# Second layer's cross attention: the key mask added by VectorE instead of by TensorE products

## The chip, the cores and the metric

The kernel runs on one core of a Trainium2 chip. The metric is the device time of one execution in microseconds (us). The engines are TensorE (PE in the profile, with its weight loads listed apart as PEld), VectorE (DVE), ScalarE (ACT), GpSimd (POOL) and SyncE (SP). SBUF is the working memory with 128 partitions, PSUM the memory that TensorE writes its results to.

## The reference, cut to what matters

The program is a decoder of two layers for 32 sequences of 64 tokens with 256 features, 2048 tokens in all. Each layer has an attention or state space part, a cross attention and a part with experts, each followed by a residual sum and a normalization. The change touches the cross attention of the second layer alone:

```python
def _L1_xattn_ref(hidden_states, memory_tokens, memory_mask, norm_w, wq, wk, wv, wo, wg):
    scale = HD ** (-0.5)                       # 16 heads of 16 features
    x = rmsnorm(hidden_states, norm_w)
    q = (x @ wq.T).reshape(B, L, NH, HD)
    k = (memory_tokens @ wk.T).reshape(B, M, NH, HD)
    v = (memory_tokens @ wv.T).reshape(B, M, NH, HD)
    attn = jnp.einsum('blhd,bmhd->bhlm', q, k) * scale
    attn = jnp.where(memory_mask[:, None, None, :], attn, -jnp.inf)
    attn = jax.nn.softmax(attn, axis=-1)
    attn = jnp.nan_to_num(attn, nan=0.0)
    out = jnp.einsum('bhlm,bmhd->blhd', attn, v).reshape(B, L, C)
    out = out @ wo.T
    gate = jax.nn.sigmoid(x @ wg.T)
    return gate * out
```

The key mask has one entry for each sequence and key (32 x 64). It is the same for all 16 heads and all queries of a sequence.

## The kernel before, in words

The parts of the decoder run one after the other, each in a block of its own that all engines leave together. `layer1_cross_attention` works on 16 tiles of 128 tokens, two sequences each. The scores of a tile are 128 x 1024 float32: a query in each partition, and along the columns 16 heads of 64 keys. They fill two banks of PSUM (`eps_s`), of which there is one copy only, so the scores of the next tile can't be written before those of this one have been read.

The order is written out by hand as a software pipeline. `for s in range(SLOTS)` runs over 22 slots on each engine, and slot `s` holds work on tiles of several ages. On TensorE a slot is: scores of tile s-1 (`scores`), queries and keys of tile s (`queries_keys`, `eps_qk`), the transposes of the mixed values of s-4 (`turn_y`), the transposes of the attention weights of s-2 (`weights`, `eps_pt`), values and gate of s (`values_gate`, `eps_vg`), the mixing of values of s-3 (`mix`, `eps_y`), the output projection of s-4 (`output`, `eps_o`) and the transposes of the normalized rows of s-5 back to feature order (`turn_back`). Slots 1 to 16 have scores, and 17 to 21 drain the pipeline.

On VectorE a slot is `softmax` of s-1 (maximum L2293, a floor under it L2295, the subtraction L2299), `apply` of s-5 (normalization L2305), `quotient` of s-3 (L2311 to L2317) and `sums` of s-4 (L2325 to L2333). On ScalarE: `turned_out` of s-6 (L2224), `exps` of s-2 (exponential L2231), the queries and keys out of PSUM for s (L2238, L2241), the turned weights out for s-2 (L2247), the mixed values out for s-4 (L2253), a square for s+1 (L2220) and values and gate out for s (L2262, L2266). GpSimd takes powers of -1/2 for the two normalizations (L2190, L2199). All engines but TensorE's weight load go strictly in order, and a semaphore stands wherever one engine takes what another made.

The mask is a bfloat16 tile `e_neg` (128 x 16 tiles x 64 keys) made once at the start (L2339): 0 for a key that counts and -1e30 for one that doesn't. In `scores` two products with the identity write it into the two banks, 512 columns each, repeated over the heads (L2381), and eight products of queries and keys (L2386) accumulate onto it. `eps_s` is released by the semaphore `shifted` of the subtraction, since maximum and subtraction both read it. `e_sm` (two copies, SBUF, float32) holds the subtracted scores until the exponential has read them.

Of the kernel before, what the change touches and what calls it, by code (L numbers as in the profile page):

```python
# [20 lines left out]
ALU = mybir.AluOpType  # L21
ACT = mybir.ActivationFunctionType
AX = mybir.AxisListType
ds = bass.ds

P = 128
B, T, D = 32, 64, 256
# [34 lines left out]
class Kernel:  # L62
# [23 lines left out]
    def sem(self, name):  # L86
        self.sems.append(self.nc.alloc_semaphore(name=name))
        return self.sems[-1]
# [2051 lines left out]
def layer1_cross_attention(k, w):  # L2140
# [4 lines left out]
    nc, io, sem = k.nc, k.io, k.sem  # L2145
    RMS_EPS, FLOOR, TINY = 1e-6, -1e20, 1e-30
    PAIRS, GD = HEADS // 2, 2 * (HD + 1)
    with ExitStack() as ctx:
# [7 lines left out]
        neg = sb("neg", [P, TILES, T], BF16)  # L2156
# [3 lines left out]
        sm, mx, pr, pt = many(2, "sm", [P, 16, T]), many(2, "mx", [P, 16]), many(2, "pr", [P, 8, P]), many(2, "pt", [P, 8, P])  # L2160
        total, yn, yT = many(2, "total", [P, 16]), many(2, "yn", [P, 16, HD]), many(2, "yT", [P, KD, P])
        r, stats, mv, rstd = many(2, "r", [P, D]), many(2, "stats", [P, 6]), many(2, "mv", [P, 2]), many(2, "rstd", [P, 1])
        qk_ps, vg_ps = k.ps("eps_qk", [P, 4, P], F32, ctx), k.ps("eps_vg", [P, 2, D], F32, ctx)
        s_ps, pt_ps = k.ps("eps_s", [P, 2, 512], F32, ctx), k.ps("eps_pt", [P, 8, P], F32, ctx)
# [2 lines left out]

        pre_done, squared, biased, fac_done = sem("e_pre_done"), sem("e_squared"), sem("e_biased"), sem("e_fac_done")
        vbd_zero, vbd_set = sem("e_vbd_zero"), sem("e_vbd_set")
        qk_full, qT_out, kbd_out = sem("e_qk_full"), sem("e_qT_out"), sem("e_kbd_out")  # L2170
        vg_full, vg_out = sem("e_vg_full"), sem("e_vg_out")
        s_full, max_done, floored, shifted, exped = sem("e_s_full"), sem("e_max_done"), sem("e_floored"), sem("e_shifted"), sem("e_exped")
# [7 lines left out]
        def live(t):  # L2180
            return 0 <= t < TILES

        with nc.Block() as block:
# [103 lines left out]
            @block.vector  # L2287
            def _(dve):
                def softmax(t):
                    v = t % 2  # L2290
                    s = s_ps[:].rearrange("p r (h s) -> p (r h) s", s=T)
                    dve.wait_ge(s_full, t + 1)
                    dve.tensor_reduce(mx[v][:], s, AX.X, ALU.max).then_inc(max_done, 1)  # L2293
                    dve.wait_ge(max_done, t + 1)
                    dve.tensor_scalar(mx[v][:], mx[v][:], FLOOR, None, ALU.max).then_inc(floored, 1)  # L2295
                    dve.wait_ge(floored, t + 1)
                    if t >= 2:
                        dve.wait_ge(exped, t - 1)
                    dve.tensor_tensor(sm[v][:], s, mx[v][:].unsqueeze(2).broadcast_to([P, 16, T]), ALU.subtract).then_inc(shifted, 1)  # L2299

                def apply(t):
                    v = t % 2
                    dve.wait_ge(rstd_done, t + 1)
                    dve.wait_ge(squared, min(t + 2, TILES))
                    dve.tensor_scalar(k.resid[:, t, :], r[v][:], mv[v][:, 0:1], rstd[v][:], ALU.subtract, ALU.mult).then_inc(rn_done, 1)  # L2305

                def quotient(t):
                    v = t % 2
                    y = y_ps[:, 0:16 * (HD + 1)].rearrange("p (h d) -> p h d", d=HD + 1)
                    dve.wait_ge(y_full, t + 1)  # L2310
                    dve.tensor_scalar(total[v][:], y[:, :, HD], TINY, None, ALU.max).then_inc(total_done, 1)  # L2311
                    dve.wait_ge(total_done, t + 1)
                    dve.reciprocal(total[v][:], total[v][:]).then_inc(rc_done, 1)
                    dve.wait_ge(rc_done, t + 1)
                    if t >= 2:
                        dve.wait_ge(y_turned, t - 1)
                    dve.tensor_tensor(yn[v][:], y[:, :, 0:HD], total[v][:].unsqueeze(2).broadcast_to([P, 16, HD]), ALU.mult).then_inc(y_out, 1)  # L2317

                def sums(t):
                    v = t % 2  # L2320
                    dve.wait_ge(o_full, t + 1)
                    dve.wait_ge(vg_out, 3 * (t + 1))
                    if t >= 2:
                        dve.wait_ge(rn_done, t - 1)
                    dve.scalar_tensor_tensor(r[v][:], gate[t % 6][:], 1.0, o_ps, ALU.add, ALU.mult).then_inc(o_out, 1)  # L2325
                    dve.wait_ge(o_out, t + 1)
                    dve.tensor_tensor(r[v][:], r[v][:], k.resid[:, t, :], ALU.add).then_inc(r_done, 1)
                    dve.wait_ge(r_done, t + 1)
                    dve.bn_stats(stats[v][:], r[v][:]).then_inc(stats_done, 1)
                    dve.wait_ge(stats_done, t + 1)  # L2330
                    if t >= 2:
                        dve.wait_ge(rstd_done, t - 1)
                    dve.bn_aggr(mv[v][:], stats[v][:]).then_inc(mv_done, 1)  # L2333

                dve.wait_ge(k.ahead_in, 16 * len(k.ahead))
                for kd in range(KD):
                    dve.tensor_scalar(wq[:, kd, :], wq[:, kd, :], nw[:, kd:kd + 1], 0.5, ALU.mult, ALU.mult).then_inc(pre_done, 1)
                    dve.tensor_scalar(wg[:, kd, :], wg[:, kd, :], nw[:, kd:kd + 1], None, ALU.mult).then_inc(pre_done, 1)
                dve.tensor_scalar(neg[:], mask8[:], -1.0, BIG, ALU.add, ALU.mult).then_inc(pre_done, 1)  # L2339
                dve.tensor_scalar(wo[:], wo[:], 0.5, None, ALU.mult).then_inc(pre_done, 1)  # L2340
                for s in range(SLOTS):
                    if live(s - 1):
                        softmax(s - 1)
                    if live(s - 5):
                        apply(s - 5)
                    if live(s - 3):
                        quotient(s - 3)
                    if live(s - 4):
                        sums(s - 4)

            @block.tensor
            def _(pe):
# [22 lines left out]
                def scores(t):  # L2375
                    pe.wait_ge(kbd_out, 4 * (t + 1))
                    pe.wait_ge(qT_out, t + 1)
                    if t >= 1:
                        pe.wait_ge(shifted, t)
                    for r2 in range(2):  # L2380
                        pe.matmul(s_ps[:, r2, :], k.identb[:], neg[:, t, :].unsqueeze(1).broadcast_to([P, 8, T]), start=True, stop=False)  # L2381
                    for r2 in range(2):
                        rows = slice(r2 * 64, r2 * 64 + 64)
                        for hh in range(2):
                            for b in range(2):
                                ins = pe.matmul(s_ps[b * T:(b + 1) * T, r2, hh * 256:(hh + 1) * 256],  # L2386
                                                qT[t % 2][rows, hh, b * T:(b + 1) * T],
                                                kbd[t % 2][rows, hh * 2 + b, :, :].rearrange("p h s -> p (h s)"),
                                                start=False, stop=(hh == 1))
                    ins.then_inc(s_full, 1)  # L2390

                def weights(t):
# [677 lines left out]
```

## Time and profile before

| | us |
|---|---|
| median of three runs | 1281.39 |
| lowest and highest | 1274.37, 1285.85 |
| the profiled execution | 1271.11 |
| its span, first to last instruction | 1269.0 |
| busy in it: TensorE | 1112.9 (88%) |
| VectorE | 781.2 (62%) |
| ScalarE | 575.9 (45%) |
| GpSimd | 455.1 (36%) |

The mean granted clock of TensorE is 0.958 of full speed. The busy times are those of one profiled execution; an engine with a small share may still be the one that the others wait for in one part of the program. The part with the cross attention of the second layer takes from about 828 to 985.87 us of the span. In the rows further down, "x16" counts instructions, and "idle before <-" is the time in which the engine had nothing to do just before the instruction, with what released it.

### The profile page before, as it was taken

To read this page: it belongs to the slowest core of one execution; us is meant where nothing else is said; L and a number is where in the kernel's file an instruction comes from. 1 tells how busy PE (TensorE), PEld (TensorE's weight loads), DVE (VectorE), ACT (ScalarE), POOL (GpSimd) and SP (SyncE) were. 2 spreads that over 40 slices of the span, in tenths; PEclk is the share of its full clock that TensorE was granted. 3 is DMA by queue.
4 is the path that set the end of the run, shared out by engine and by line. 5 is a ranking of instruction groups with operands and counts; after the bars stand their busy time and mean duration, and the time that the engine had idled before them with its cause. 6 is when DMAs were issued, how large, how long until landed. Compare 5 with 4: busy or idle time off the path is not lost. (4 is left out here: it accounts for less than half of the span.)

```text
span 1269.0 us, 20972 instructions
## 1 busy us (share of the span) xinstructions
PE 1112.9 (88%) x7484; PEld 662.5 (52%) x7484; DVE 781.2 (62%) x1531; ACT 575.9 (45%) x1199; POOL 455.1 (36%) x692
## 2 busy tenths in 40 slices
PE   6888779988888588999579998789998899999997
PEld 3566544454443245776234455567786343545455
DVE  4889887888884322333667677736566355555554
ACT  2666516766677301333455664256664322122120
POOL 6999852545542263333224445421111000000001
PEclk7999969999999799999789999989999899999999
DMA  6658244655652023333323000000000000000000
GB/s 217 202 174 275 81 124 122 150 137 148 146 130 53 25 84 96 105 109 101 99 65 141 1 1 1 1 1 2 2 2 1 25 1 0 9 9 9 8 9 25
DMA packets 73115, 91.72 MB, mean 72 GB/s; under 512 B 12691, under 2 KB 61997, under 8 KB 72333
## 3 DMA queue, kind: packets, MB, share of 16 engines
q1 hardware_dynamic: 68595, 80.72, 22.6%
q0 software_dynamic: 3408, 9.34, 2.1%
q8 instruction: 62, 1.02, 0.4%
q10 hardware_dynamic: 1010, 0.31, 0.1%
q14 instruction: 40, 0.33, 0.1%
HBM read 55.37 MB, written 29.17 MB: 67 GB/s over the span
## 5 line engine op out<-in xcount | busy, mean ns | idle before, releaser
L919 ACT ACTIVATE a_late<-a_qkv 128x512 f32<-128x512 f32 x128 | 77.2, 603 | 58.9 <-PE a_qkv L996 58.9
L2546 POOL TENSOR_SCALAR f_rstd<-f_mv 128x1 f32<-128x1 f32 x16 | 3.8, 240 | 267.9 <-DVE f_mv L2685 267.8
L867 DVE TENSOR_REDUCE b_nm<-a_s 128x4 f32<-128x1024 f32 x64 | 78.0, 1219 | 29.9 <-PE a_s L965 29.8
L2630 DVE TENSOR_TENSOR f_prod<-f_sg,f_kept 128x512 f32<-128x512 f32 (+1 forms) x48 | 33.2, 692 | 97.9 <-ACT f_kept L2575 95.0
L2755 PE MATMUL fps_h<-residT,w_f_w 128*128 128x512 f32 x176 | 83.9, 617 | 2.4 <-DVE f_inner L2667 2.4
L867 DVE TENSOR_REDUCE b_nm<-a_pt 128x4 f32<-128x1024 f32 x64 | 76.7, 1198 | 1.5 <-PE a_pt L965 1.5
L919 ACT ACTIVATE a_late<-a_y 128x512 f32<-128x512 f32 x128 | 76.9, 600 | 0.0
L2569 ACT ACTIVATE f_sg<-fps_h 128x512 f32<-128x512 f32 (+1 forms) x24 | 14.3, 596 | 126.6 <-PE fps_h L2774 109.8
L1011 PE MATMUL a_o<-a_late,b_vt 128*32 128x256 f32 x1024 | 69.2, 389 | 0.0
L1299 POOL DMA_INDIRECT routed<-c_out,c_target x39 | 37.5, 962 | 67.4 <-ACT c_out L1371 67.1
L1888 DVE SCALAR_TENSOR_TENSOR d_acc<-d_pad,d_cw,d_acc 128x512 f32<-128x512 f32 x72 | 57.8, 810 | 1.7
L351 POOL TENSOR_TENSOR a_nrm<-a_ss,phalf 128x20 f32<-128x20 f32 x16 | 57.0, 3560 | 4.2 <-DVE a_ss L473 4.2
L2755 PEld LDWEIGHTS fps_h<-residT,w_f_w 128*128 128x128 f32 x176 | 33.8, 196 | 42.9 <-issue 38.5
L1547 PE MATMUL cps_h<-c_wgu,c_xT 128*128 x156 | 52.7, 461 | 0.7 <-ACT c_xT L1359 0.6
L1486 DVE TENSOR_TENSOR c_hid<-c_sg,cps_h 128x176 f32<-128x176 f32 x39 | 13.2, 338 | 63.2 <-issue 50.6
L839 POOL TENSOR_TENSOR a_rest<-a_rest 128x256 f32<-128x256 f32 x16 | 11.6, 725 | 96.8 <-DVE a_rest L892 96.8
L1737 POOL TENSOR_TENSOR d_rs<-d_ms,mhalf 128x4 f32<-128x4 f32 x16 | 22.4, 1401 | 65.6 <-DVE d_ms L1945 65.6
L2011 PE MATMUL dps_ip<-residT,d_win 128*128 128x512 f32 x96 | 44.6, 598 | 0.3 <-ACT d_zs L1798 0.2
L1293 POOL DMA_INDIRECT xrows<-c_xr,c_place_int x32 | 31.1, 971 | 34.6 <-DVE c_xr L1456 19.3
L2569 ACT ACTIVATE f_sg<-f_kept 128x512 f32<-128x512 f32 (+1 forms) x24 | 15.1, 630 | 60.1 <-DVE f_kept L2635 60.1
L1566 PE MATMUL cps_o<-c_wd,c_hT 88*128 x156 | 40.1, 380 | 0.0
L1011 PEld LDWEIGHTS a_o<-a_late,b_vt 128*32 128x32 f32 x1024 | 26.9, 110 | 25.1 <-issue 14.0
(425 smaller groups left out, 2895.8 us busy)
## 6 DMA issues: line engine op xcount, KB each, us to landing
kparts<-a_rest SPq DMA_DIRECT2D x48, 192.0 KB, 3.2
a_rest<-a_rest SPq DMA_DIRECT2D x64, 128.0 KB, 3.1
xrows<-in_c_fill SPq DMA_DIRECT2D x13, 387.0 KB, 4.4
c_xrow<-xrows SPq DMA_DIRECT2D x39, 129.0 KB
c_back<-routed SPq DMA_DIRECT2D x16, 256.0 KB, 3.3
a_front<-kparts SPq DMA_DIRECT2D x12, 288.0 KB
a_front<-qparts SPq DMA_DIRECT2D x36, 96.0 KB
qparts<-b_xp SPq DMA_DIRECT2D x48, 64.0 KB, 2.8
```

Source lines behind the costliest of these rows:

```text
L351: gp.tensor_tensor(nrm[v][:], ss[v][:], k.phalf[:, 0:H20], ALU.pow).then_inc(rooted, 1)
L867: dve.tensor_reduce(nm[s % 2][:, 4 * n:4 * n + 4].rearrange("p (g h) -> p g h", h=2), s1[step % 2][:], AX.X, ALU.max, negate=True).then_in ...
L919: act.activation(pr[g % 8][:], s2[g % 2][:], ACT.Exp, scale=SCALE).then_inc(s2_out, 1)
L1011: ins = pe.matmul(o_ps[32 * j:32 * j + 32, q % 2, :], vt[x % 2][:, lh, g, :], pr[g % 8][:, lh, :], start=(lh == 0), stop=(lh == KD - 1))
L1293: gp.indirect_dma_start(k.xrows[:], bass.IndirectOffsetOnAxis(ap=place_int[n][:, t:t + 1], axis=0), xr[:, t, :], None).then_inc(scattered[ ...
L1299: gp.indirect_dma_start(routed[:], bass.IndirectOffsetOnAxis(ap=target[s % 8][:], axis=0), out[s % 4][:], None).then_inc(sent[s % 4], 16)
L1547: ins = pe.matmul(h_ps[s % 2][:, 0:2 * F], xT[s % 2][:, kd, :], wgu[:, kd, ds(e, 1), :].rearrange("p a f -> p (a f)"), start=(kd == 0), st ...
L1566: ins = pe.matmul(o_ps[:, s % 2, 0:D], hT[s % 2][:, c, :], wd2[:, ds(e, 1), c, :].rearrange("p a f -> p (a f)"), start=(c == 0), stop=(c = ...
L1888: ins = dve.scalar_tensor_tensor(out=acc[v][:], in0=pad[v][:, :, tap:tap + T], scalar=cw[:, m, tap:tap + 1], in1=acc[v][:], op0=ALU.mult, ...
L2011: ins = pe.matmul(bank[:], win[:, kd, m * P:(m + 1) * P] if m < XT else wz[:, kd, (m - XT) * P:(m - XT + 1) * P], k.residT[:, kd, c * CHUN ...
L2630: dve.tensor_tensor(prod[n % 2][at], sg[n % 2][at], up, ALU.mult).then_inc(prod_done, 1)
L2755: pe.matmul(h_ps[j][:], (w1, w3)[j][:, kd, m * P:(m + 1) * P], k.residT[:, kd, c * CHUNK:(c + 1) * CHUNK], start=(kd == 0), stop=False)
```

## The change

The two mask products of each tile go, and with them the accumulation: each product of queries and keys starts and ends its own sum. VectorE's `softmax` has a new first instruction, which reads the scores from PSUM, adds the mask repeated over the heads, and writes `e_sm`. The maximum is taken from `e_sm`, and the subtraction works in place on `e_sm`. A new semaphore `masked` is raised by the addition; TensorE waits for it, in place of `shifted`, before it writes the next scores. The wait for the exponential that last read this copy of `e_sm` moves from the subtraction to the addition.

```diff
         vbd_zero, vbd_set = sem("e_vbd_zero"), sem("e_vbd_set")
+        masked = sem("e_masked")
...
                 def softmax(t):
                     v = t % 2
-                    s = s_ps[:].rearrange("p r (h s) -> p (r h) s", s=T)
                     dve.wait_ge(s_full, t + 1)
-                    dve.tensor_reduce(mx[v][:], s, AX.X, ALU.max).then_inc(max_done, 1)
+                    if t >= 2:
+                        dve.wait_ge(exped, t - 1)
+                    dve.tensor_tensor(sm[v][:], s_ps[:].rearrange("p r (h s) -> p (r h) s", s=T),
+                                      neg[:, t, :].unsqueeze(1).broadcast_to([P, 16, T]), ALU.add).then_inc(masked, 1)
+                    dve.wait_ge(masked, t + 1)
+                    dve.tensor_reduce(mx[v][:], sm[v][:], AX.X, ALU.max).then_inc(max_done, 1)
                     dve.wait_ge(max_done, t + 1)
                     dve.tensor_scalar(mx[v][:], mx[v][:], FLOOR, None, ALU.max).then_inc(floored, 1)
                     dve.wait_ge(floored, t + 1)
-                    if t >= 2:
-                        dve.wait_ge(exped, t - 1)
-                    dve.tensor_tensor(sm[v][:], s, mx[v][:].unsqueeze(2).broadcast_to([P, 16, T]), ALU.subtract).then_inc(shifted, 1)
+                    dve.tensor_tensor(sm[v][:], sm[v][:], mx[v][:].unsqueeze(2).broadcast_to([P, 16, T]), ALU.subtract).then_inc(shifted, 1)
...
                     if t >= 1:
-                        pe.wait_ge(shifted, t)
-                    for r2 in range(2):
-                        pe.matmul(s_ps[:, r2, :], k.identb[:], neg[:, t, :].unsqueeze(1).broadcast_to([P, 8, T]), start=True, stop=False)
+                        pe.wait_ge(masked, t)
...
-                                                start=False, stop=(hh == 1))
+                                                start=True, stop=True)
```

On TensorE, around the scores of tile 7 in slot 8, the instructions stand like this before (output projection, transposes back, mask, scores, queries, keys):

```order
L2425 MATMUL eps_o<-w_e_wo,e_yT 128x256 x2
L2434 MATMUL eps_pt<-ident,resid 128x128 x2
L2381 MATMUL eps_s<-e_neg,identb 128x512 x2
L2386 MATMUL eps_s<-e_kbd,e_qT 64x256 x8
L2359 MATMUL eps_qk<-residT,w_e_wq 128x128 x4
L2359 MATMUL eps_qk<-ctxT_all,w_e_wk 128x128 x4
```

and like this after:

```order
L2426 MATMUL eps_o<-w_e_wo,e_yT 128x256 x2
L2435 MATMUL eps_pt<-ident,resid 128x128 x2
L2387 MATMUL eps_s<-e_kbd,e_qT 64x256 x8
L2362 MATMUL eps_qk<-residT,w_e_wq 128x128 x4
L2362 MATMUL eps_qk<-ctxT_all,w_e_wk 128x128 x4
```

The scores follow the transposes back directly; nothing else has moved.

On VectorE, at the same place, before (the last two of `sums`, then `softmax`, `apply` and the first of `quotient`):

```order
L2329 BN_STATS e_stats<-e_r 128x6
L2333 BN_AGGR e_mv<-e_stats 128x2
L2293 TENSOR_REDUCE e_mx<-eps_s 128x16
L2295 TENSOR_SCALAR e_mx<-e_mx 128x16
L2299 TENSOR_TENSOR e_sm<-eps_s,e_mx 128x1024
L2305 TENSOR_SCALAR resid<-e_r,e_mv,e_rstd 128x256
L2311 TENSOR_SCALAR e_total<-eps_y 128x16
```

and after:

```order
L2332 BN_STATS e_stats<-e_r 128x6
L2336 BN_AGGR e_mv<-e_stats 128x2
L2295 TENSOR_TENSOR e_sm<-eps_s,e_neg 128x1024
L2298 TENSOR_REDUCE e_mx<-e_sm 128x16
L2300 TENSOR_SCALAR e_mx<-e_mx 128x16
L2302 TENSOR_TENSOR e_sm<-e_sm,e_mx 128x1024
L2308 TENSOR_SCALAR resid<-e_r,e_mv,e_rstd 128x256
L2314 TENSOR_SCALAR e_total<-eps_y 128x16
```

The addition stands ahead of the maximum, and is now the only instruction that reads `eps_s`.

## Rows read from the trace of the kernel before

**Rows 1.** Windows: start:end, length, busy time per engine, granted clock, DMA share, GB/s.

```profile
core 0: us, PE busy (x) PEld busy (x) DVE busy (x) ACT busy (x) POOL busy (x), PEclk, DMA share, GB/s
837.25:964.87 127.62, 127.62 (x1434) 100.97 (x1433) 70.43 (x141) 85.73 (x203) 19.12 (x51) 1.00 0.01 2
965.90:985.87 19.97, 12.93 (x150) 9.47 (x147) 12.50 (x33) 6.39 (x13) 3.93 (x10) 1.00 0.00 1
985.87:989.00 3.13, 3.13 (x16) 0.66 (x16) 0.00 (x0) 0.00 (x0) 0.00 (x0) 0.50 0.64 217
989.00:1269.00 280.00, 267.25 (x764) 132.44 (x760) 150.98 (x279) 63.69 (x116) 12.90 (x32) 0.98 0.03 8
```

**Rows 2.** Timeline (start, length, engine, line) of TensorE around the mask, steady slots.

```profile
901.25 0.59 PE L2381 MATMUL eps_s<-e_neg,identb 128*128 128x512 bf16 x2
...
910.04 0.38 PE L2434 MATMUL eps_pt<-ident,resid 128*128 128x128 f32 x2
910.16 0.21 PEld L2381 LDWEIGHTS eps_s<-e_neg,identb 128*128 128x128 bf16 x2
...
910.26 0.59 PE L2381 MATMUL eps_s<-e_neg,identb 128*128 128x512 bf16 x2
...
910.79 0.65 PEld L2386 LDWEIGHTS eps_s<-e_kbd,e_qT 64*64 64x64 f32 x16 [0.42 <-issue]
```

**Rows 3.** Timeline of VectorE in the same slot.

```profile
909.20 0.17 DVE L2311 TENSOR_SCALAR e_total<-eps_y 128x16 f32<-128x16 f32 x1 [3.21 <-PE eps_y L2410]
...
911.62 0.18 DVE L2333 BATCH_NORM_AGGREGATE e_mv<-e_stats 128x2 f32<-128x6 f32 x1
...
911.98 1.23 DVE L2293 TENSOR_REDUCE e_mx<-eps_s 128x16 f32<-128x1024 f32 x1 [0.18 <-PE eps_s L2386]
...
914.59 0.40 DVE L2305 TENSOR_SCALAR resid<-e_r,e_mv,e_rstd 128x256 f32<-128x256 f32 x1
```

**Rows 4.** Groups of VectorE instructions by form: total us, mean ns, idle before.

```profile
L2656 DVE TENSOR_TENSOR f_hid<-f_aw 128x512 f32<-128x512 f32 x20 | 13.8, 690 | 0.6
...
L499 DVE TENSOR_TENSOR a_front<-a_front,a_sc 128x256 f32<-128x256 f32 x16 | 11.8, 738 | 0.0
...
L1392 DVE TENSOR_TENSOR c_acc<-cps_o,resid 128x1024 f32<-128x1024 f32 x4 | 4.9, 1213 | 5.6 <-PE cps_o L1528 5.6
```

**Rows 5.** Timeline in the fill: the exponential and the transposes that need it.

```profile
843.72 1.14 ACT L2231 ACTIVATE e_pr<-e_sm,e_fac 128x1024 f32<-128x1024 f32 x1
...
845.77 1.04 PE L2399 MATMUL eps_pt<-ident,e_pr 128*128 128x128 f32 x8
```

**Rows 6.** Timeline of slot 16 and of the drain behind it.

```profile
964.83 1.14 ACT L2231 ACTIVATE e_pr<-e_sm,e_fac 128x1024 f32<-128x1024 f32 x1
...
965.70 0.18 DVE L2333 BATCH_NORM_AGGREGATE e_mv<-e_stats 128x2 f32<-128x6 f32 x1
...
966.06 1.22 DVE L2293 TENSOR_REDUCE e_mx<-eps_s 128x16 f32<-128x1024 f32 x1 [0.18 <-PE eps_s L2386]
...
966.18 1.04 PE L2399 MATMUL eps_pt<-ident,e_pr 128*128 128x128 f32 x8
...
968.67 0.40 DVE L2305 TENSOR_SCALAR resid<-e_r,e_mv,e_rstd 128x256 f32<-128x256 f32 x1
...
969.57 0.38 PE L2434 MATMUL eps_pt<-ident,resid 128*128 128x128 f32 x2
...
970.27 1.14 ACT L2231 ACTIVATE e_pr<-e_sm,e_fac 128x1024 f32<-128x1024 f32 x1
...
971.47 1.09 PE L2399 MATMUL eps_pt<-ident,e_pr 128*128 128x128 f32 x8 [0.68 <-ACT e_pr L2231]
```

**Rows 7.** First attention, by source line (lengths in ns: least, median, most) and timeline.

```profile
L495 DVE TENSOR_TENSOR a_sc<-a_sc,a_factor x16: 167/643/649, 19.8 to 146.9; 128x20 f32<-128x20 f32 x16
...
102.71 0.80 POOL L362 TENSOR_TENSOR a_front<-a_front,a_rest 128x256 f32<-128x256 f32 x1
102.90 0.64 DVE L495 TENSOR_TENSOR a_sc<-a_sc,a_factor 128x20 f32<-128x20 f32 x1
```

## The prediction

> **What bounds the kernel now.** I looked at the windows by stage first, then at the timeline of one steady slot, then at where the pipeline fills and drains. The part that the change touches is the cross attention of the second layer, from about 828 us to 985.87 us. Between the first and the last score product TensorE is busy for 127.62 of 127.62 us, VectorE for 70.43 and ScalarE for 85.73, at full granted clock; after that the pipeline drains for 19.97 us, in which TensorE is busy for only 12.93 [rows 1]. So in the steady part TensorE's own instruction stream is the bound, and an instruction taken from it should shorten every slot. In the drain the bound is a chain that goes from engine to engine, and there VectorE's work counts.
>
> The timeline shows a steady slot: the mask products start at 901.25 and again at 910.26, so a slot is 9.01 us [rows 2]. Within it VectorE waits 3.21 us for the mixed values, and its last statistics of the slot end at 911.62 + 0.18 = 911.80, hardly before the maximum starts at 911.98 [rows 3]. The second number matters: scores that come earlier will not be picked up much earlier, since VectorE is still at work.
>
> **What is removed: two products of TensorE per tile, 32 in all.** The transposes back start at 910.04, the mask's weights at 910.16, its first product at 910.26, and the scores' first weights at 910.79 [rows 2]. Without the mask the scores can start where the mask started. From its first product that is 910.79 - 910.26 = 0.53 us, from its first weights 910.79 - 910.16 = 0.63. I take 0.53, because a first product there still has to have weights in the array, and the scores' first weights need to be loaded just as the mask's were. Below lies the case that the idle 0.42 us of the weight load ahead of the scores stays (it would then be a price of the switch to the small tiles of the scores, not of the mask): 0.63 - 0.42 = 0.21. The bounds are 0.21 and 0.63.
>
> The same row can be read another way. The Trainium skill, "TensorE: Matmul & The Clock Gate", section "Back-to-back issue gap", gives N/2.4 + 2.5 ns from one product's start to the next at full clock, so an estimate of 216 ns for each of these 512-column products and 0.43 for the two. By it the sum below would be 15 x 0.43 - 0.73 = 5.7 us of gain. The row has 0.53, which also holds the weight load that stands ahead, and I go by the row.
>
> **What is added on VectorE: one addition of 1024 columns per tile, 16 in all.** It reads the scores in PSUM and the mask in SBUF, and writes SBUF. The nearest row is a float32 sum of the same size with one operand in each memory, at 1213 ns [rows 4]; this trace has no row for a bfloat16 operand in such a sum, nor for one repeated over the heads. The highest price by a row is that of a product with a repeated operand, 738 ns for 256 columns [rows 4]; by the rows of 512 and 1024 columns an instruction costs 1.02 ns per column and 168 ns besides, so this one has (738 - 168)/256 = 2.2 ns per column, which for 1024 would be 2.45 us. At that price VectorE would still fit into the slot, and the drain alone would be 1.2 us longer. I take 1.22, and 0.04 for the semaphore behind it. Nothing below 1.2 is to be had. The maximum and the subtraction then read SBUF in place of PSUM. The 690 ns for 512 columns are those of a product with both operands in SBUF, and they lie on one line with the sum that has one in PSUM [rows 4]; I change nothing for them.
>
> VectorE in a slot is at work for 9.01 - 3.21 - 0.18 = 5.62 us. With the addition it is 5.62 + 1.26 = 6.88, and the slot of TensorE becomes 9.01 - 0.53 = 8.48. **So 1.6 us of idle VectorE remain in each slot**, and the addition is hidden. Who waits for VectorE there? The scores' PSUM is now free after the addition: that starts at about 911.85 and ends at 913.1, and the next scores come six microseconds later. The subtraction ends 1.1 us later than now, and behind it on VectorE's queue stands the normalization, now at 914.59 [rows 3], which the transposes back need only at the slot's end. None of it is late. The exponentials take the subtraction's result one slot later.
>
> What could come late on ScalarE is the exponential ahead of TensorE's transposes of the weights, since TensorE gains 0.53 between the two. In the fill, where it is tightest, it ends at 843.72 + 1.14 = 844.86, while TensorE's first transpose is at 845.77 and its weights 0.1 ahead of that [rows 5]. Of these 0.8 us, 0.53 go and 0.27 stay. In the steady slot there is more.
>
> **The drain.** In slot 16, the last with scores, two things are different. First, the exponential of tile 14 ends at 964.83 + 1.14 = 965.97 and the transposes start at 966.18 [rows 6], with their weights 0.1 earlier, so that TensorE can not use the sixteenth 0.53. Second, the chain now goes through VectorE: its statistics end at 965.88, the maximum starts at 966.06, the normalization at 968.67; behind that the transposes back at 969.57, behind these in ScalarE's queue the exponential at 970.27, and behind it the transposes at 971.47, where TensorE had waited 0.68 [rows 6]. With the addition ahead, everything from the maximum on is 1.26 later, less the 0.13 by which the addition starts earlier (965.93): 1.13. The normalization at 969.80 ends at 970.21, the transposes back start at 970.30 in place of 969.57, which is 0.73 later, and the exponential and the transposes with it. From there the drain keeps its form. So the drain costs 0.73.
>
> **The sum.** 15 x 0.53 - 0.73 = 7.95 - 0.73 = 7.2 us of gain. The profiled execution took 1271.11 us with a span of 1269.0, and would be 1263.9. The median of the three runs is 1281.39, 10 above it; that difference is the spread between executions, of which the three runs show 1274.37 to 1285.85. From the median I get 1281.4 - 7.2 = **1274 us**.
>
> **The rivals.**
>
> *The gap ahead of the scores stays.* For it: a gap of this size is put down to "issue" in the row, not to an engine [rows 2]. Against it: while that gap runs, two products of 512 columns are streaming. Gain 15 x 0.21 - 0.73 = 2.4 us, 1279 us. Chance 0.13. (Were that gap itself all that goes, and the mask's weight load found its like in the scores', it would be 15 x 0.42 - 0.73 = 5.6 us and 1276, which I count to the forecast.)
>
> *The clock is dealt anew.* Right behind the drain the granted clock is 0.50 for 3.13 us, the lower of its two levels, after a drain with TensorE at 65% busy; over the last 280 us it is 0.98 on average [rows 1]. The end of the drain is now stretched by 0.73 and everything later moves by 7 us, so a fall can come earlier, or once more. One more such stretch of dense products costs half its length, 1.6 us; two cost 3.1. The result would be 1276 to 1277, or as much better if one goes away. Chance 0.08.
>
> *VectorE becomes the bound.* This is the way to a slower kernel. Its place is the steady slot; it decides when the addition takes more than 8.48 - 5.66 = 2.8 us, and the kernel is slower than before only above 3.4 us in the slots, since a slot was 9.01. At 4.0 us a slot would be 9.66, and 13 slots cost 13 x 0.65 = 8.4, and the drain 4.04 - 0.13 - 0.41 = 3.5 more: 12 us, 1293. Against it: no row of this size is above 1.23, and even the worst row gives 2.45. Chance 0.03.
>
> *The subtraction, now with both operands in SBUF, is held up by GpSimd.* The first attention shows such a thing: a product of 128x20 with both operands in SBUF, which takes 167 ns at least, took 640 at 102.90, and ended just behind GpSimd's subtraction of 102.71 to 103.51 [rows 7]. The price here would be the length of GpSimd's operation, up to 0.8 us per tile by that row. VectorE has 1.6 us to spare in a slot, so it would be seen in the drain alone, once: gain 7.2 - 0.8 = 6.4, 1275. By my times the subtraction stands at 914.6 to 915.8, and GpSimd's power for this slot's normalization has ended by then, since VectorE's normalization at 914.59 waited for nothing [rows 3]. Chance 0.04. The Trainium skill, "SBUF — State Buffer", section "Who interferes with whom", states the rule behind it: a VectorE instruction with two SBUF inputs contends with a GpSimd instruction that reads SBUF, and the second waits in full. The rows agree. It speaks against this change, which turns a subtraction with one SBUF input into one with two.
>
> The rest, 0.72, is the forecast.
>
> **Numbers.** The costs alone give gains from 2.4 to 15 x 0.63 - 0.73 = 8.7, so 1273 to 1279; the clock adds 3 on either side. The larger part of the range is the spread of the executions, 11 us over three runs, half of which I allow to a median: 1265 to 1282. About 1% (13 us) is what a measurement of this kernel can tell from no change. A gain of 7 is 0.6%, so within 1% is by far the likeliest; more than 1% faster needs 6 us of luck in the executions, 0.14; more than 1% slower needs VectorE as the bound, 0.03.
>
> **What would show it.** In the profile of the changed kernel the starts of successive scores in the steady part should lie 8.48 us apart, with the scores' first weights directly behind the transposes back and no idle time of TensorE. The addition should read 1.22 us, VectorE's longest wait in a slot should fall from 3.21 to about 1.5, and stay for the mixed values. The drain should take some 20.7 us and not 19.97 from the end of the last scores, with TensorE waiting more for the last exponential. I am wrong if the slots are 8.8 us or more (the gap stayed), if TensorE waits in a steady slot for VectorE or ScalarE (a wait has taken the place of the products), or if the granted clock in the steady part is below 1.00.

## The result, and the profile after

The changed kernel takes 1272.42 us in the median of 20 runs (1267.85 to 1279.63), the kernel before 1277.82 in 20 runs on the same chips (1273.03 to 1286.44). The ratio is 0.996, with a 95% interval of 0.9943 to 0.9976: a gain of 0.4%, or 5.1 us, between 3.1 and 7.3. That is within 1% and in the range of 1265 to 1282, and below the 7.2 us of the forecast.

The spans of the two profiled executions, 1269.0 and 1268.4 us, don't show this. The stage's first product of queries starts at 830.23 before and at 834.35 after; over all profiled executions of this study it starts between 829.68 and 841.75, though no kernel changes the stages ahead of it. So I compare from that product on. Windows of the changed kernel: from the first product of queries to the first scores, to the last scores, to the first product of the experts, to the next products there, to the end.

```profile
core 0: us, PE busy (x) PEld busy (x) DVE busy (x) ACT busy (x) POOL busy (x), PEclk, DMA share, GB/s
834.35:840.88 6.53, 6.53 (x37) 5.75 (x38) 0.00 (x0) 2.24 (x7) 3.54 (x15) 0.60 0.01 3
840.88:961.90 121.02, 121.02 (x1403) 98.50 (x1402) 87.28 (x155) 85.53 (x201) 19.53 (x51) 1.00 0.01 2
961.90:984.10 22.20, 14.59 (x164) 9.95 (x164) 14.99 (x38) 7.73 (x14) 3.92 (x10) 0.97 0.00 1
984.10:987.67 3.57, 3.57 (x17) 0.65 (x17) 0.00 (x0) 0.00 (x0) 0.00 (x0) 0.50 0.62 220
987.67:1268.40 280.73, 268.08 (x764) 132.68 (x760) 151.04 (x279) 63.68 (x116) 12.84 (x32) 0.98 0.02 8
```

The same windows of the kernel before:

```profile
830.23:837.26 7.03, 7.03 (x39) 6.00 (x39) 0.00 (x0) 2.51 (x8) 4.04 (x15) 0.62 0.01 2
837.26:964.87 127.61, 127.61 (x1434) 100.96 (x1433) 70.43 (x141) 85.72 (x203) 19.11 (x51) 1.00 0.01 2
964.87:985.87 21.00, 13.96 (x163) 10.03 (x163) 13.45 (x36) 7.42 (x14) 3.93 (x10) 1.00 0.00 1
985.87:989.33 3.46, 3.46 (x16) 0.66 (x17) 0.00 (x0) 0.00 (x0) 0.00 (x0) 0.53 0.64 221
989.33:1269.00 279.67, 266.92 (x764) 132.44 (x760) 150.98 (x279) 63.69 (x116) 12.90 (x32) 0.98 0.02 8
```

The reader is to see three things. The stretch from the first to the last scores, 15 slots, is 6.59 us shorter, 0.44 per slot, and TensorE is still busy in all of it, while VectorE has 17 us more to do. The drain is 1.20 longer. The first stretch is 0.50 shorter, but that isn't to be put down to the change: it runs in part at the lower clock (0.60 and 0.62), and the kernel with products and addition further down, whose mask products are those of before, takes 6.16 us for it. So the stage takes 984.10 - 834.35 = 149.75 us in place of 155.64, 5.9 less, and what is behind it 1.2 more.

One steady slot of the changed kernel, TensorE and VectorE, in answer to [rows 2, 3]:

```profile
901.83 1.11 PE L2387 MATMUL eps_s<-e_kbd,e_qT 64*64 64x256 f32 x16
...
909.25 0.17 DVE L2314 TENSOR_SCALAR e_total<-eps_y 128x16 f32<-128x16 f32 x1 [1.80 <-PE eps_y L2411]
...
910.10 0.38 PE L2435 MATMUL eps_pt<-ident,resid 128*128 128x128 f32 x2
...
910.41 0.65 PEld L2387 LDWEIGHTS eps_s<-e_kbd,e_qT 64*64 64x64 f32 x16 [0.17 <-issue]
...
911.68 0.18 DVE L2336 BATCH_NORM_AGGREGATE e_mv<-e_stats 128x2 f32<-128x6 f32 x1
911.78 1.20 DVE L2295 TENSOR_TENSOR e_sm<-eps_s,e_neg 128x1024 f32<-128x1024 f32 x1
...
913.01 1.22 DVE L2298 TENSOR_REDUCE e_mx<-e_sm 128x16 f32<-128x1024 f32 x1
...
914.48 1.23 DVE L2302 TENSOR_TENSOR e_sm<-e_sm,e_mx 128x1024 f32<-128x1024 f32 x1
...
915.62 0.41 DVE L2308 TENSOR_SCALAR resid<-e_r,e_mv,e_rstd 128x256 f32<-128x256 f32 x1
```

A slot is 910.41 - 901.83 = 8.58 us. From the transposes back to the scores it is 0.31 us, where it was 0.75. The addition takes 1.20 us and starts right behind the statistics, and VectorE's longest wait has gone from 3.21 to 1.80.

### The profile page after: what moved, and what is told of

Read it like the earlier page. It is cut to its first block and busy times, and to the rows that moved or that the text cites. A ratio compares the mean times of both kernels' runs of the same rounds, so it can differ in the third digit from the quotient of the medians.

```text
span 1268.4 us, 20924 instructions
## 1 busy us (share of the span) xinstructions
PE 1113.3 (88%) x7452; PEld 663.0 (52%) x7452; DVE 801.8 (63%) x1547; ACT 575.7 (45%) x1199; POOL 453.0 (36%) x692
```

## The experiments

Each run's profile is read in the same four pieces. "Slots" is the time from the first to the last scores (15 of them), "drain" from the last scores to the experts' first product, "stage" from the first product of queries to the experts' first. All in us:

| kernel | slots | drain | stage | ratio to before |
|---|---|---|---|---|
| before | 127.62 | 21.00 | 155.64 | 1 |
| changed | 121.03 | 22.20 | 149.75 | 0.996 (0.9943 to 0.9976) |
| products and addition | 127.61 | 22.12 | 155.89 | 1.0004 (0.9976 to 1.0033) |
| neither | 121.03 | 21.58 | 149.17 | 0.9939 (0.9907 to 0.9971) |
| one product | 124.37 | 21.11 | 152.30 | one run |
| four products | 134.10 | 21.00 | 162.72 | one run |
| two additions | 121.04 | 27.17 | 154.84 | 1.0 (0.997 to 1.0029) |
| three additions | 126.97 | 27.68 | 161.10 | 1.0048 (1.002 to 1.0075) |
| two additions, spare products | 121.03 | 23.89 | 151.24 | 0.9969 (0.9946 to 0.9991) |
| changed, normalization earlier | 121.03 | 21.65 | 149.18 | 0.9964 (0.9939 to 0.999) |
| changed, spare products | 121.04 | 24.45 | 151.48 | 0.9936 (0.9912 to 0.996) |
| factor on the values | 121.22 | 21.33 | 149.27 | 0.9936 (0.9908 to 0.9965) |
| the same, nine spare products | 121.22 | 24.46 | 152.04 | 0.995 (0.9929 to 0.997) |
| the same, three spare products | 121.22 | 21.76 | 149.75 | 0.9938 (0.9915 to 0.996) |

### The two halves of the change apart

Both, the products back and the addition kept:

```diff
                         pe.wait_ge(masked, t)
+                    for r2 in range(2):
+                        pe.matmul(s_ps[:, r2, :], k.identb[:], neg[:, t, :].unsqueeze(1).broadcast_to([P, 8, T]), start=True, stop=False)
...
-                                                start=True, stop=True)
+                                                start=False, stop=(hh == 1))
```

> Changed kernel, but the two mask products of TensorE are put back ahead of the scores (the mask is then added twice). Theory (each slot is as long as TensorE's own stream, and the addition costs in the drain alone): slots of 9.01 us as in the kernel before, from the last scores to the next stage 21.0 + 0.76 = 21.8 us, the whole stage 156.4 us against 155.6 before; about 0.8 us slower than before, not to be told from no change. Rival (the addition lengthens the slots as well, and the products are worth more than 0.43 us): slots of 9.2 us or more, 3 us slower or more.

The slots take 127.61 us, as before to the hundredth, with VectorE doing the addition in each of them. The drain is 1.12 longer than before, where 0.8 was expected, and the time is that of before (1.0004). About 0.25 of the 1.12 stand at its end, where the clock falls earlier: the last transposes back take 0.69 us in place of 0.44. The stage is only 0.25 longer, since its first stretch happened to be 0.87 shorter. So the addition costs nothing in the slots, and 0.9 to 1.1 in the drain.

Neither, from the kernel before (the key mask is left out of the computation):

```diff
-                    for r2 in range(2):
-                        pe.matmul(s_ps[:, r2, :], k.identb[:], neg[:, t, :].unsqueeze(1).broadcast_to([P, 8, T]), start=True, stop=False)
...
-                                                start=False, stop=(hh == 1))
+                                                start=True, stop=True)
```

> Neither the mask products nor the addition: the key mask is left out. Theory: slots of 8.58 us as in the changed kernel, since VectorE was hidden there; from the last scores to the next stage 21.35 us against 22.20 of the changed kernel; stage 148.9 us, 0.85 below the changed kernel and 6.7 below before. Rival (VectorE's addition holds the slots a little): slots below 8.55 us, stage below 148 us.

The slots are 121.03 us, as in the changed kernel; the drain is 21.58, where 21.35 was expected, and 0.62 below the changed one. Of the two kernels the whole difference is in the drain. The ratios, 0.9939 and 0.996, go the same way, but their intervals overlap.

### What one product costs

```diff
-                    for r2 in range(2):
+                    for r2 in range(1):
                         pe.matmul(s_ps[:, r2, :], k.identb[:], neg[:, t, :].unsqueeze(1).broadcast_to([P, 8, T]), start=True, stop=False)
...
-                                                start=False, stop=(hh == 1))
+                                                start=(r2 == 1), stop=(r2 == 1 or hh == 1))
```

> Kernel before with the mask product of the first bank alone; the eight heads of the second bank are left without a mask. Theory (the products cost what they stream, 0.215 us each, and nothing for the switch): slots of 8.58 + 0.215 = 8.80 us. Rival (0.1 us is a fixed price of a first product ahead of the scores, as the 0.53 us in the row of the kernel before suggested): the first product costs more than the second, slots of 8.85 us or more.

```diff
-                    for r2 in range(2):
-                        pe.matmul(s_ps[:, r2, :], k.identb[:], neg[:, t, :].unsqueeze(1).broadcast_to([P, 8, T]), start=True, stop=False)
+                    for again in range(2):
+                        for r2 in range(2):
+                            pe.matmul(s_ps[:, r2, :], k.identb[:], neg[:, t, :].unsqueeze(1).broadcast_to([P, 8, T]), start=True, stop=(again == 0))
```

> Kernel before with the two mask products issued twice. Theory (each product costs its streaming of 0.215 us): slots of 9.01 + 0.43 = 9.44 us, stage 155.6 + 16 x 0.43 = 162.5 us. Rival (a weight load or a wait per product stands on the path too): slots of 9.5 us or more.

With none, one, two and four products the slots are 121.03, 124.37, 127.62 and 134.10 us. Per slot that is 0.223 for the first, 0.217 for the second and 0.216 each for the third and fourth. There is no fixed price of a first product to speak of (steady slots of 8.58, 8.80, 9.01 and 9.45 us), so the theory of streaming holds. The Trainium skill's formula that was weighed in the prediction ("TensorE: Matmul & The Clock Gate", section "Back-to-back issue gap") is for the gap of a single product and gives 216 ns, and these runs have it in a full stream; the 131 ns that the same section states for a stream of such products is not what they show.

### How much VectorE can take

```diff
         masked = sem("e_masked")
+        again = sem("e_again")
...
                     dve.wait_ge(masked, t + 1)
+                    dve.tensor_tensor(sm[v][:], sm[v][:], neg[:, t, :].unsqueeze(1).broadcast_to([P, 16, T]), ALU.add).then_inc(again, 1)
+                    dve.wait_ge(again, 1 * t + 1)
                     dve.tensor_reduce(mx[v][:], sm[v][:], AX.X, ALU.max).then_inc(max_done, 1)
```

> Changed kernel with a second addition of the mask on VectorE, in place in SBUF. Theory: VectorE is busy 6.78 + 1.26 = 8.04 us of a slot, TensorE's 8.58 still set it; only the drain grows by 1.25 to 23.4 us; stage 151.0 us. Rival (the order of the queues makes VectorE late already, or an addition with both operands in SBUF collides with GpSimd): slots of 8.7 us or more, additions of over 1.3 us.

The slots are as expected, 121.04 us. The drain is not: 27.17 us in place of 23.4. The next section is on that. With one more addition of the same form behind it:

> Changed kernel with two more additions on VectorE. Theory: VectorE needs 6.78 + 2.52 = 9.30 us for a slot and becomes the bound: slots of 9.3 us, TensorE idle 0.7 in each, drain 24.7 us, stage 161 us, 6 us slower than before (1.005). Rival (a chain through several engines adds to it): slots of 9.6 us or more. If VectorE were not the bound at 9.3, slots would stay at 8.58.

VectorE is the bound now, but at a lower price than I expected: one steady slot of this kernel, TensorE's scores of two slots and its wait for the normalization.

```profile
904.76 1.11 PE L2392 MATMUL eps_s<-e_kbd,e_qT 64*64 64x256 f32 x16
...
913.37 0.44 PE L2440 MATMUL eps_pt<-ident,resid 128*128 128x128 f32 x2 [0.18 <-DVE resid L2313]
...
913.73 1.11 PE L2392 MATMUL eps_s<-e_kbd,e_qT 64*64 64x256 f32 x16
```

A slot is 8.97 us, not 9.30, and VectorE has no wait left in it (busy 8.63 of 8.97). The 6.78 us that I had taken as VectorE's work in the changed kernel was all the time outside its longest wait, and held shorter gaps that go when VectorE is late. Without waits three additions take 8.97, so one takes about 8.97 - 2 x 1.26 = 6.45, and VectorE had 2.1 us to spare in a slot of 8.58.

The expected stage of 161 us and ratio of 1.005 were met (161.10, 1.0048 with its interval above 1), but by luck: the slots cost less than expected and the drain, 27.68 us in place of 24.7, 3.0 more. The slots alone are still 0.6 us shorter than in the kernel before (126.97 against 127.61), and the stage is longer because the drain is 6.7 longer. So even three additions per tile don't lose in the slots; they lose in the drain.

### Why two additions cost 5 us

TensorE in the drain of that kernel: the transposes back of slot 16 and 17, and the transposes of the weights between them. Then the granted clock there.

```profile
969.00 0.44 PE L2438 MATMUL eps_pt<-ident,resid 128*128 128x128 f32 x2 [1.74 <-DVE resid L2311]
...
970.95 1.97 PE L2403 MATMUL eps_pt<-ident,e_pr 128*128 128x128 f32 x8
...
976.57 0.63 PE L2438 MATMUL eps_pt<-ident,resid 128*128 128x128 f32 x2
```

```profile
968.00:970.00 2.00, 0.44 (x2) 0.20 (x2) 1.93 (x6) 0.53 (x2) 0.00 (x0) 0.88 0.00 0
970.00:980.00 10.00, 9.54 (x83) 7.52 (x84) 4.32 (x14) 2.96 (x5) 1.57 (x4) 0.50 0.01 2
980.00:982.00 2.00, 2.00 (x6) 1.45 (x6) 0.86 (x4) 0.00 (x0) 0.00 (x0) 0.50 0.00 0
```

TensorE waited 1.74 us for the normalization behind the long softmax, and worked 0.44 of the 2 us from 968 to 970. At the end of that its clock fell to the lower level, 1.2 GHz, and stayed there for over 12 us, in which the eight transposes took 1.97 us where they take 1.04. The kernel with three additions has the same: a wait of 3.42 us at this place, and the lower clock behind it.

```profile
976.00:986.00 10.00, 8.59 (x60) 6.24 (x62) 5.16 (x17) 3.39 (x6) 0.78 (x2) 0.50 0.01 2
```

To tell a cause from a companion I gave TensorE products in the waits of the kernel with two additions, whose results nobody reads:

```diff
+                def spare(count):
+                    for n in range(count):
+                        pe.matmul(qk_ps[:].rearrange("p a b -> p (a b)"), wk[:, 0, 0:P], k.ctxT[:, 0, 0:512], start=True, stop=True)
...
+                    if s == TILES + 1:
+                        spare(1)
                     if live(s - 4):
                         turn_y(s - 4)
...
+                    if s == TILES:
+                        spare(3)
                     if live(s - 5):
                         turn_back(s - 5)
```

> The kernel with two additions, with spare products in TensorE's waits of the drain: three of 512 columns ahead of slot 16's transposes back (where it waited 1.74 us) and one in slot 17; nobody reads them. In that kernel the granted clock fell to 0.50 at about 969.8 us and the drain was 27.2 us in place of the 23.4 expected. Theory (the fall comes from TensorE having had little to do there): the clock stays at 1.00 until the last slots, drain 23.5 us, stage 151.1 us in place of 154.8. Rival (the drain is longer through the order on VectorE, and the clock only follows): drain stays at 27 us.

```profile
975.00:985.00 10.00, 8.34 (x94) 5.76 (x92) 5.99 (x19) 3.87 (x7) 1.56 (x4) 1.00 0.01 2
```

The clock stays at 1.00 and the drain is 23.89, though TensorE has more to do and VectorE's order is the same. The stage is 3.6 us shorter than with the two additions alone. That the idle stretch made the clock fall is shown for this place by these profiles, one of each kernel; the runs (0.9969 against 1.0, with intervals that overlap) don't tell the two apart. The Trainium skill says the same of cause and effect ("TensorE: Matmul & The Clock Gate", section "What's actually happening": the throttled state is the default, and activity releases it). A long wait alone doesn't say when it falls: the kernel before waits 2.44 us for its last transposes back, and these still run at 1.00.

### The drain, and the start of the experts

In slot 16 alone, the normalization is put between the addition and the maximum:

```diff
+                    if between is not None:
+                        apply(between)
                     dve.wait_ge(masked, t + 1)
...
-                    if live(s - 1):
-                        softmax(s - 1)
-                    if live(s - 5):
-                        apply(s - 5)
+                    last = s == TILES
+                    if live(s - 1):
+                        softmax(s - 1, s - 5 if last else None)
+                    if live(s - 5) and not last:
+                        apply(s - 5)
```

> Changed kernel, but in slot 16, the last with scores, VectorE does the normalization of tile 11 between the addition and the maximum of tile 15, in place of behind the subtraction. Theory (the drain is held by what is queued behind VectorE's softmax of slot 16): slots unchanged at 8.58 us, the transposes back no longer wait for it, the last exponential comes 0.6 us earlier and TensorE's transposes of it 0.4; from the last scores to the next stage 21.8 in place of 22.2 us. In total 0.4 us below the changed kernel, less than the runs can tell. Rival (the drain's growth comes from the late exponential of tile 14 or from elsewhere): drain stays at 22.2 us.

The drain is 21.65 us, 0.55 below the changed kernel, where 0.4 was expected; the runs (0.9964) can't tell it from the changed kernel, as foreseen. The transposes back start 5.03 us behind the last scores' start in place of 5.67. That the normalization behind softmax holds the drain is shown by the trace.

With spare products in the drain of the changed kernel (the edit above, with one in slots 16, 17 and 19, four in slot 20, two at the end):

> The changed kernel with spare products in TensorE's waits of the drain (one in slots 16, 17 and 19, four in slot 20, two behind the last transposes back); nobody reads them. Theory (the clock is at 0.50 at the start of the experts because TensorE is nearly idle in the last slots): the experts' first 16 products take 1.8 us in place of 3.6 and the products behind them run at full clock; 2 us below the changed kernel, 0.994 to 0.995 of before. Rival (the clock there depends on other things): 3.6 us again, same time as the changed kernel.

The experts' first 16 products, in the changed kernel and here:

```profile
984.10 3.64 PE L2823 MATMUL fps_o<-residT,w_f_gw 128*32 128x512 f32 x16 [0.73 <-PEq L2184]
```

```profile
981.61 3.60 PE L2440 MATMUL eps_qk<-ctxT_all,w_e_wk 128*128 128x512 f32 x8
985.04 0.38 PE L2435 MATMUL eps_pt<-ident,resid 128*128 128x128 f32 x2
985.26 1.88 PE L2440 MATMUL eps_qk<-ctxT_all,w_e_wk 128*128 128x512 f32 x4
987.44 1.92 PE L2836 MATMUL fps_o<-residT,w_f_gw 128*32 128x512 f32 x16 [0.30 <-PEq L2184]
```

They take 1.92 us in place of 3.64: the clock held. But a spare product is two instructions in the rows, 0.86 us, and four of them fill 3.4 us where the wait was 2.43. With the two at the end, which stand ahead of the experts for 1.1 us, the drain is 2.25 longer. In the profile the gain and the loss about cancel up to the products behind (153.3 us from the stage's first product in both, though this kernel's first stretch was 0.5 shorter). The runs put it at 0.9936 against 0.996, with intervals that overlap; a gain over the changed kernel isn't shown.

### A version without the addition

The experiments above say that the slots want nothing more on TensorE and the drain nothing on VectorE's softmax. Masked keys can also be left out behind the softmax: a factor of 0 or 1 on the values and in the column of ones that sums the weights. The mask products and the floor under the maximum go as well; the cut shows what comes in their place.

```diff
-        neg = sb("neg", [P, TILES, T], BF16)
+        keep = sb("keep", [P, TILES, 2])
...
+                def kept_keys(t):
+                    ...
+                    for h2 in range(2):
+                        rows = slice(h2 * T, (h2 + 1) * T)
+                        ...
+                        gp.tensor_copy(vbd[t % 4][rows, :, :, h2, HD], keep[rows, t, :].unsqueeze(2).broadcast_to([T, 2, PAIRS])).then_inc(vbd_set, 1)
...
-                        act.activation(vbd[t % 4][rows, :, :, h2, 0:HD], values[rows], ACT.Copy).then_inc(vg_out, 1)
+                        for b in range(2):
+                            act.activation(vbd[t % 4][rows, b, :, h2, 0:HD], values[rows, b], ACT.Copy, scale=keep[rows, t, b:b + 1]).then_inc(vg_out, 1)
```

> No mask on the scores at all: the masked keys are left out behind the softmax, by a factor of 0 or 1 per key that ScalarE multiplies onto the values as it takes them from PSUM (four copies of 64x128 in place of two of 64x256) and that GpSimd writes into the column of ones that sums the weights. The floor under the maximum is left out, which it then doesn't need, and in slot 16 the normalization stands ahead of the subtraction. Theory (TensorE's stream sets the slots, VectorE's softmax the drain): slots of 8.58 us, drain 21.1 us, stage 148.7 us, 1.0 below the changed kernel; 0.995 of before. Rival (ScalarE's or GpSimd's added work is not hidden): slots of 8.7 us or more, slower than the changed kernel.

The slots take 121.22 us, 0.19 more than in the changed kernel, all of it in the second and third slot of the fill; the steady slots are 8.58 as expected, so there the added copies of ScalarE and GpSimd are hidden. The drain is 21.33 where 21.1 was expected, the stage 149.27 where 148.7 was, and the first product of queries starts 0.5 earlier, since the factor is made faster than the mask was (its wait is 2.58 us in place of 3.08). The ratio is 0.9936 (0.9908 to 0.9965). Its median, 1267.0 us, is the shortest, but the ratio is that of the changed kernel with spare products, and its lead over the changed kernel is 1.0 us in the traces; more than that isn't shown.

Its two companions with spare products:

> The kernel with the factor on the values, and the spare products of the changed kernel with spare products. Theory: both gains add up, stage 148.5 us, the experts' first 16 products 1.8 us; 0.993 of before, 4 us below the changed kernel. Rival: the spare products hold up the drain, whose waits are shorter here, and the sum is no better than with either alone.

> The kernel with the factor on the values, with fewer spare products: two in slot 20, where TensorE waits 2.43 us, and one behind the last transposes back. A spare product takes 0.86 us (two passes of 0.43), so eight or nine of them were more than the waits hold: that kernel's drain was 24.5 us in place of 21.3. Theory: the drain stays at 21.3 to 21.6 us, the clock stays up, the experts' first 16 products take 1.9 us; stage 149.4 us, and the experts' h products start 1.5 us earlier after its start; 0.992 of before. Rival (three products are too few to keep the clock up): the first 16 products take 3.5 us as without.

With nine the drain is 24.46 and the ratio 0.995, not better than with either alone, as the rival said. With three the drain is 21.76, 0.4 above, and the clock held:

```profile
986.50 1.92 PE L2841 MATMUL fps_o<-residT,w_f_gw 128*32 128x512 f32 x16 [0.30 <-PEq L2183]
...
999.32 3.59 PE L2793 MATMUL fps_h<-f_inner,w_f_b 128*128 128x512 f32 x4 [0.44 <-DVE f_inner L2686]
```

The first 16 products take 1.92 us as expected, and the experts' next products start 151.6 us after the stage's first, against 152.7 without spare products, 1.1 earlier where 1.5 was expected. But the ratio is not 0.992; it is 0.9938, that of the kernel without them: at 999.32, behind the next short waits, four instructions take 3.59 us, twice the 1.88 that four of this size take at full clock. The two other kernels whose clock held at the start of the experts show the same fall at this place (0.57 and 0.58 on average over the 3 us behind it). That this later fall gives back what the first one had cost is argued from one profile of each kernel, not shown.

## Why the prediction was right

**The bound and its consequence: right.** TensorE's stream sets the slots, and the products are worth what they stream. With the addition and with neither, the slots are the same to 0.01 us in 121.

**The size of the first term: too large.** The step was "I take 0.53, because a first product there still has to have weights in the array, and the scores' first weights need to be loaded just as the mask's were". Measured: 0.44 per slot, 0.22 per product, so 15 x 0.09 = 1.4 us of the 7.2 were never there. The step that failed is that 0.53 was the mask's alone. Two products stream for 2 x 0.216 = 0.43 from 910.26, so up to 910.69, and the scores' first weights came at 910.79: 0.10 of the 0.53 is a gap between the end of the stream and the scores. It is still there. In the kernel before the transposes back gave way to the mask after 0.22 us (910.04 to 910.26), in the changed one the scores come 0.31 behind their start, 0.09 later. The mask's first weight load isn't it: it lay under the transposes (910.16, its product at 910.26) and cost nothing, as the nearly equal prices of the first and the second product say. So the rival of the gap that stays was right in kind and wrong in size: the idle time ahead of the scores' weights went from 0.42 to 0.17, since most of it was the mask's own stream, and about 0.09 of it goes with the scores. What the gap comes from is not shown. The other reading that the prediction gave of this row, 0.43 for the two products and 5.7 us in all, was the nearer one.

**The drain: right in mechanism; that the size is right as well is luck.** Expected was 0.73, and for the last 0.53, which TensorE can't use, the exponential of tile 14 was named. In the trace the drain from the last scores is 1.20 longer, of which 0.44 are the saving of slot 16 not used, which leaves 0.76. The sign given for it, 20.7 us from the end of the last scores, left that 0.53 out and was short: counted that way the drain took 21.2. The rows of the changed kernel, in answer to [rows 6]:

```profile
963.48 0.86 PEld L2400 LDWEIGHTS eps_pt<-ident,e_pr 128*128 128x128 f32 x8 [0.34 <-ACT e_pr L2232]
...
967.58 0.44 PE L2435 MATMUL eps_pt<-ident,resid 128*128 128x128 f32 x2 [0.48 <-DVE resid L2308]
...
968.33 1.14 ACT L2232 ACTIVATE e_pr<-e_sm,e_fac 128x1024 f32<-128x1024 f32 x1
...
969.52 1.09 PE L2400 MATMUL eps_pt<-ident,e_pr 128*128 128x128 f32 x8 [0.29 <-ACT e_pr L2232]
...
982.76 0.61 PE L2435 MATMUL eps_pt<-ident,resid 128*128 128x128 f32 x2 [2.43 <-DVE resid L2308]
```

The transposes of tile 14 now wait for the exponential, and the transposes back for the normalization, as forecast. The last row is one that was not: 0.61 in place of 0.44, since the clock falls a little earlier than it did. That is 0.17 of the 0.76, and the chain through VectorE accounts for 0.59, less than the 0.73: the addition starts 0.27 earlier than the maximum did, not 0.13.

**The addition: right.** It takes 1.20 to 1.23 us against 1.22; the bfloat16 operand repeated over the heads costs nothing. The subtraction with two operands in SBUF takes 1224 to 1226 ns in all 16 cases, so GpSimd never held it up. In the steady slots GpSimd's powers have ended before it starts, so the rival was not put to the test here. VectorE has more to spare than the 1.6 us I gave it, 2.1 by the kernel with three additions.

**The clock: open.** What lies behind the stage is 1.2 us longer in the profile, with the experts' start at the lower clock for longer: the four instructions behind the first 16 take 2.98 us (1.98 before). So in the profiles the sum is 5.9 - 1.2 = 4.7, and in the runs 5.1. That the change did this isn't shown. From the experts' first product to the end it is 283.14 us before, but 281.63 in the kernel with one product, whose drain is within 0.11 of it; over all kernels it lies between 280.01 and 284.29, and a longer drain doesn't go with a longer rest (281.40 with a drain of 21.65, 283.28 with 21.00). The kernel before has a low stretch of its own, some 68 us into the experts, which the one with one product lacks. So the clock behind the stage is dealt anew from kernel to kernel, as the rival said, and by about what it was priced at. Inside the drain it isn't luck: there VectorE's work for one more addition, 1.25 us, made it 5 longer, by the clock.

Together: 7.2 less 1.4 for the first term, and less 0 to 1.2 for the clock, is 4.6 to 5.8, and the runs show 3.1 to 7.3.

## What to carry to other kernels

When a product is taken out of a full TensorE stream, count what it streams, and don't take the time from its start to the start of what follows: a gap ahead of what follows can stay when the product is gone. Work moved to an engine with idle time is free in the steady part only: count it again where the pipeline drains, by what is queued behind it, and look at whether TensorE's clock falls in the longer wait. A stage can be compared between two profiles from its own first instruction on when what precedes it varies by more than the effect.

## What the runs showed of the hardware that I had not expected

- TensorE's clock fell after a wait of 1.74 us in the drain in a stretch where it had 0.44 of 2 us of work, and stayed at 0.50 for more than 12 us with TensorE busy for 9.54 of 10 us. In the changed kernel waits of 0.48, 0.81 and 0.29 us at the same place left it at 1.00. At the drain's end a wait of 2.44 us in the kernel before left it at 1.00 for the transposes behind it.
- The identity products cost the same, 0.216 to 0.223 us of a slot, whether there is one, two or four, while their rows show 379 ns each.
- About 0.09 us pass between the end of the stream ahead and the scores' first weights, behind the mask products and behind the transposes back alike.
- The start of this stage varies by 12 us over the profiles (829.68 to 841.75) in kernels whose stages ahead of it are alike, which is more than twice the gain measured here.
